# Two row-buffer slots of 16 batches in place of four of 8, in the plain gather passes of a graph network

## The chip, the cores and the metric

The program runs on one core of a Trainium2 chip. The metric is the device time of one execution in microseconds (us). The engines are called as in the profile: PE (TensorE, with PEld for its weight loads), DVE (VectorE), ACT (ScalarE), POOL (GpSimd) and SP (SyncE). PEq, POOLq and so on are the sequencers of these engines.

## What is computed

The reference runs four blocks on a graph of 12500 nodes and 200000 edges sorted by destination, with 128 features in fp32. Every block normalises its input, takes the positive part, and adds its result to `x`. What all of them share is a gather of source rows and a sum over destinations:

```python
def _L0_gnn_ref(x, edge_index, W0, b0, W1, b1, W2, b2):
    count = jax.ops.segment_sum(jnp.ones((src.shape[0],), dtype=x.dtype), dst, num_segments=n)
    inv = 1.0 / (count + 1.0)
    for W, b in ((W0, b0), (W1, b1), (W2, b2)):
        agg = jax.ops.segment_sum(x[src], dst, num_segments=n)
        neigh = agg * inv[:, None]
        x = jax.nn.relu(jnp.concatenate([x, neigh], axis=-1) @ W + b)
    return x
# L1: attention over the edges (softmax by destination), then a feed-forward block
# L2: segment_sum(relu(h[src] + edge_attr), dst), then two matmuls with batch norms
# L3: x + segment_sum(x[src] + edge_attr, dst)
```

## The kernel before

The sum over edges is the function `aggregate`, and the program calls it six times: `agg0`, `agg1` and `agg2` for the three layers of the first block, `agg3` for the attention, `agg4` for the third block (with edge attributes), and `agg5` for the last block. The calls `agg0`, `agg1`, `agg2` and `agg5` are the plain gather passes: rows are gathered from a table in HBM (`rows_a` or `rows_b`) and summed as they are. `agg3` reads rows that an earlier pass, `gat_gather`, has gathered on POOL and written to HBM; `agg4` gathers too, but adds edge attributes before the sum.

The 200000 edges are padded to 1568 batches of 128 edges. One batch is one indirect DMA, issued by POOL (line 680), that brings 128 rows of 128 numbers into `work`, one row per partition. Four batches form a group (`GT`). All edges of a group have destinations in one window of 64 nodes (`W`), so PE sums a group with four matmuls (line 751): the gathered rows are the weights, and a one-hot matrix of 128 edges by 64 nodes is the moving operand. DVE makes the one-hot matrices (`compare`, line 803) and adds each group's result from PSUM to `regionA` (`add`, line 846), at a column read from a table (line 837).

The loops run over 49 iterations (`NIT`) of 32 batches, which are eight groups. `work` holds the 32 batches of one iteration, and `S` says into how many slots it is divided; `ST` is the number of batches of a slot and `SG` that of its groups. The engines speak to each other per slot:

- POOL waits until PE has finished all `SG` groups of the slot in the iteration before (`summed[h]`, line 677), and then issues `ST` gathers. The wait and the increment of `moved` stand ahead of the slot's gathers in POOL's queue.
- PE waits for the one-hot matrices of the slot (line 741), for the landing of all its gathers (`gathered[h]`, line 743), and for each group for `added` (line 748): with `NB` banks of PSUM, a group can start when the group `NB` before it has been added. `NB` is 4 in the passes with a dense part (`agg0`, `agg1`, `agg2`, `agg5`) and 8 in `agg3` and `agg4`.
- DVE waits in `add` for each group's `summed[h]`, adds, and then makes the one-hot matrices of the same slot for the next iteration. In `agg0` it also sums the one-hot matrices (line 811) for the counts of edges.

`summed[h]` is incremented by PE once for each group, and both DVE and POOL wait for it. Semaphores carry the order across engines, and each engine runs its own list in order. When the sums of a chunk of 500 nodes are complete, `due_chunks` lets PE, DVE and ACT run the pass's dense part for this chunk (`Sage`, `Project` or `Finish`), between two iterations on PE, and on DVE between the last `add` and the last `compare` of an iteration. There are 25 chunks in a pass of 49 iterations.

Of the kernel before, what the change touches and what calls it, by code (L numbers as in the profile page):

```python
# [595 lines left out]
def aggregate(net, tag, table=None, extra=None, follow=None):  # L596
# [12 lines left out]
    attention, edges = extra == "attention", extra == "edges"  # L609
    width = XW if attention else D  # L610

    S = 2 if attention or edges else 4
    ST, SG = 2 * HALF // S, 2 * GPH // S
    rows = [net.work[:, h * ST * XW:h * ST * XW + ST * width] for h in range(S)]
    rows3 = [r.rearrange("p (t f) -> p t f", f=width) for r in rows]
    attr = [net.B[:, h * HALF * D:(h + 1) * HALF * D] for h in range(2)]

    piles = [net.C[:, REG + h * SG * W:REG + (h + 1) * SG * W] for h in range(S)]
    onehot = net.onehot[:, :, :, :].rearrange("p a t w -> p (a t) w")
# [12 lines left out]
    bank_of = lambda h, q, k: net.psum[0:high[k], (h * SG + q) % NB * 512 + k * W:(h * SG + q) % NB * 512 + (k + 1) * W]  # L632
    name = lambda k: [net.sem(f"{tag}_{k}{h}") for h in range(S)]
    index_ready = net.sem(f"{tag}_index")
    onehot_ready = name("onehot")
    gathered = name("gathered") if attention else [net.pool_sem() for _ in range(S)]
    summed = name("summed")
# [7 lines left out]
    with nc.Block() as block:  # L645
# [5 lines left out]
        if not attention:  # L651
# [12 lines left out]
            def _(pool):  # L664
# [3 lines left out]
                with pool.Fori(0, R) as r:  # L668
                    def gather(i, k):

                        n = pool.snap(r * NIT + i)
                        pool.wait_ge(index_ready, r * staged + i + 1)  # L672
                        for h in range(S):
                            if edges:
# [1210 lines left out]
def program(nc, dram, out):  # L1885
    with ExitStack() as ctx:
        net = Net(nc, ctx, dram)
        allocate(net)
        for step in (
                lambda: prepare(net),  # L1890

                lambda: normalise(net, "n0", first=True, table=net.TA),
                lambda: aggregate(net, "agg0", net.TA, "count",
                                  Sage(net, "sage0", "L0_gnn_W0", "L0_gnn_b0", net.TB, first=True)),
                lambda: aggregate(net, "agg1", net.TB, None,
                                  Sage(net, "sage1", "L0_gnn_W1", "L0_gnn_b1", net.TA)),
                lambda: aggregate(net, "agg2", net.TA, None, Project(net, "project")),

                lambda: gat_gather(net),
                lambda: gat_softmax(net),  # L1900
                lambda: gat_begin(net),
                lambda: aggregate(net, "agg3", extra="attention", follow=Shares(net, "shares")),
                lambda: gat_output(net),

                lambda: normalise(net, "n2", keep=True, table=net.TB),
                lambda: aggregate(net, "agg4", net.TB, "edges"),
                lambda: gin_output(net),

                lambda: normalise(net, "n3", table=net.TA),
                lambda: aggregate(net, "agg5", net.TA, None, Finish(net, "finish", out))):  # L1910
            with net.stage():
                step()
# [27 lines left out]
```

## Time and profile before

| | |
|---|---|
| time, median of 3 runs | 17063.85 us (16991.23 to 17120.43) |
| profiled execution | 16898.69 us, span of its instructions 16896.7 us |
| POOL busy | 9578.3 us (57%) |
| PE busy, PEld busy | 6796.4 us (40%), 5870.2 us (35%) |
| DVE busy, ACT busy | 3299.2 us (20%), 824.4 us (5%) |
| granted TensorE clock, mean | 0.529 of full speed |
| data moved | 1124.64 MB, mean 67 GB/s |

The stretches of the span, from the first gather of a pass to the start of what follows: `agg0` 296 to 2600 us, `agg1` 2600 to 4897, `agg2` 4897 to 7260, `gat_gather` 7299 to 9470, then the softmax, `agg3` from about 10235, the attention's output and a normalisation, `agg4` 11730 to 14260, and `agg5` 14618 to the end. The four plain passes are 9243 us of 16897. POOL is busy in each for about two thirds; the rest of its time is the gap between two gathers and the waits at the start of a slot. An average over the whole span hides this, since POOL does nothing in `agg3`.

### The profile page before, as it was taken

The page shows a single profiled execution, that of the slowest core. Times are in us where ns is not written, and L with a number is a line of the kernel's source. Part 1 is how long each engine was busy: PE and PEld are TensorE (multiplying, and loading weights), DVE is VectorE, ACT ScalarE, POOL GpSimd, SP SyncE. Part 2 cuts the span into 40 slices and gives each one's busy share as a digit, 9 for nine tenths or more (in the row PEclk, how much of TensorE's full clock was granted, in tenths as well). Part 3 has the DMA queues.
Part 4 walks back from the last instruction along what each step waited for, and adds up shares of the span by engine and source line. Part 5 has one row for each costly group of instructions (what it writes and reads, how often), then busy time and mean ns, then how long its engine had stood idle before and what let it go on. Part 6 is the DMA issues. An engine that isn't in the chain of part 4 may idle for free. (4 is left out here: it accounts for less than half of the span.)

```text
span 16896.7 us, 120575 instructions
## 1 busy us (share of the span) xinstructions
PE 6796.4 (40%) x30243; PEld 5870.2 (35%) x30244; DVE 3299.2 (20%) x6637; ACT 824.4 (5%) x1247; POOL 9578.3 (57%) x9860
## 2 busy tenths in 40 slices
PE   3444443333333444310000009996555555533333
PEld 2434333333333333200000008873555555333333
DVE  3222221111111222100000014444111112311111
ACT  1000000000000000000000000003000000200000
POOL 2666666666666666667777440001666664366666
PEclk8555555555555555555555555557555555655555
DMA  2111111111111222133333212222222222221212
GB/s 85 48 48 48 48 47 46 48 47 49 48 47 53 58 56 57 53 86 100 100 100 99 68 33 82 100 92 82 79 85 83 83 79 90 67 55 53 55 52 53
DMA packets 593156, 1124.64 MB, mean 67 GB/s; under 512 B 220826, under 2 KB 364385, under 8 KB 566579
## 3 DMA queue, kind: packets, MB, share of 16 engines
q0 software_dynamic: 307488, 624.42, 14.6%
q1 hardware_dynamic: 285622, 499.73, 8.8%
q8 instruction: 15, 0.25, 0.0%
q14 instruction: 31, 0.25, 0.0%
HBM read 904.32 MB, written 218.95 MB: 66 GB/s over the span
## 5 line engine op out<-in xcount | busy, mean ns | idle before, releaser
L680 POOL DMA_INDIRECT work<-rows_a,index x4704 | 4544.1, 966 | 2425.0 <-issue 1475.6
L751 PE MATMUL psum<-onehot,work 128*128 128x64 f32 x12544 | 2864.0, 416 | 3649.9 <-issue 1191.6
L680 POOL DMA_INDIRECT work<-rows_b,index x3136 | 3088.4, 985 | 1771.2 <-issue 1039.4
L751 PEld LDWEIGHTS psum<-onehot,work 128*128 128x128 f32 x12544 | 2721.0, 325 | 3797.5 <-issue 2795.1
L1191 POOL DMA_INDIRECT work<-attention_rows,index x1568 | 1608.7, 1026 | 610.6 <-issue 559.1
L751 PE MATMUL psum<-onehot,regionB 128*128 128x64 f32 x6272 | 1550.0, 417 | 720.8 <-issue 564.0
L751 PEld LDWEIGHTS psum<-onehot,regionB 128*128 128x128 f32 x6272 | 1438.7, 327 | 816.6 <-issue 789.8
L846 DVE TENSOR_TENSOR regionA<-regionA,psum 128x64 f32 x2352 | 508.7, 216 | 5116.3 <-remote 3598.3
L765 PE MATMUL psum<-onehot,regionB 128*4 128x64 f32 (+1 forms) x6272 | 1171.4, 358 | 467.2 <-issue 466.5
L765 PEld LDWEIGHTS psum<-onehot,regionB 128*4 128x4 f32 (+1 forms) x6272 | 1021.7, 224 | 516.9 <-issue 470.5
L182 POOL COPY work<-regionB 128x500 f32 (+1 forms) x75 | 45.3, 603 | 2030.6 <-DVE regionB L561 2030.6
L843 DVE TENSOR_TENSOR regionC<-regionC,psum 128x64 f32 (+1 forms) x1176 | 254.3, 216 | 3573.1 <-remote 2273.1
L1339 PE MATMUL psum<-ident,work 128*128 128x128 f32 x49 | 18.3, 452 | 2213.9 <-POOL work L1294 2213.7
L803 DVE TENSOR_TENSOR onehot<-rel_n,window 128x512 f32<-128x512 f32 (+1 forms) x980 | 779.4, 796 | 272.6 <-issue 263.3
L1339 PEld LDWEIGHTS psum<-ident,work 128*128 128x128 f32 x49 | 8.9, 182 | 2223.3 <-POOL work L1294 2220.9
L162 DVE CAST index<-src_n (+1 forms) x301 | 56.6, 189 | 2251.2 <-DMA work<-attention_rows,index 2073.2
L969 PE MATMUL psum<-regionB,weights 128*128 x100 | 101.5, 1118 | 790.1 <-DVE regionA L959 623.0
L831 DVE TENSOR_TENSOR regionB<-work,regionB 128x2048 f32<-128x2048 f32 x98 | 225.0, 2295 | 470.5 <-DMA regionB<-in_edge_attr 256.4
L661 ACT ACTIVATE regionB<-regionB 128x2048 f32<-128x2048 f32 x98 | 187.1, 1910 | 2383.8 <-DVE regionB L831 1808.8
L969 PEld LDWEIGHTS psum<-regionB,weights 128*128 128x128 f32 x100 | 25.1, 311 | 799.2 <-issue 799.2
L756 PE MATMUL psum<-regionC,ones 128*128 128x64 f32 x784 | 243.8, 404 | 135.6 <-issue 126.8
L1001 PE MATMUL psum<-ident,turn 128*125 128x128 f32 x300 | 77.7, 403 | 547.7 <-issue 306.5
(253 smaller groups left out, 4638.8 us busy)
## 6 DMA issues: line engine op xcount, KB each, us to landing
gathered_rows<-work SPq DMA_DIRECT2D x98, 1088.0 KB
work<-gathered_rows SPq DMA_DIRECT2D x98, 1088.0 KB, 4.9
regionB<-in_edge_attr SPq DMA_DIRECT2D x195, 512.0 KB
work<-rows_a,index POOLq DMA_INDIRECT x4704
work<-rows_b,index POOLq DMA_INDIRECT x3136
work<-attention_rows,index POOLq DMA_INDIRECT x1568
x_transposed<-regionA SPq DMA_DIRECT2D x75, 250.0 KB, 6.0
rows_a<-regionC SPq DMA_DIRECT2D x50, 250.0 KB
```

The costliest lines, as they stand in the source:

```text
L661: nc.scalar.activation(msgs[h], msgs[h], ACT.Relu).then_inc(relued[h], 1)
L680: pool.indirect_dma_start(rows3[h][:, t, :], None, table, bass.IndirectOffsetOnAxis(ap=net.index[:, k, h * ST + t:h * ST + t + 1], axis=0) ...
L751: last = nc.tensor.matmul(bank_of(h, q, 0), msgs3[h][:, t, 0:D], onehot[:, h * ST + t, :], start=(k == 0), stop=(k == GT - 1))
L756: last = nc.tensor.matmul(bank_of(h, q, 1), net.ones[:, :], piles[h][:, q * W:(q + 1) * W], start=True, stop=True)
L765: last = nc.tensor.matmul(bank_of(h, q, 1), lhs, onehot[:, h * ST + t, :], start=(k == 0), stop=(k == GT - 1))
L803: nc.vector.tensor_tensor(onehot[:, h * ST:(h + 1) * ST, :], net.rel_n[:, bass.ds(i * 2 * HALF + h * ST, ST)].unsqueeze(2) .broadcast_to([ ...
L831: nc.vector.tensor_tensor(msgs[h], rows[h], attr[h], ALU.add).then_inc(message[h], 1)
L843: nc.vector.tensor_tensor(Cc[0:high[1], bass.ds(at, W)], Cc[0:high[1], bass.ds(at, W)], bank_of(h, q, 1), ALU.add)
L846: nc.vector.tensor_tensor(A[:, bass.ds(at, W)], A[:, bass.ds(at, W)], bank_of(h, q, 0), ALU.add).then_inc(added, 1)
L969: net.nc.tensor.matmul(dense(net, 0), self.w[:, 0:D], net.col(net.B, c), start=True, stop=False)
L1001: t = net.nc.tensor.transpose(net.psum[0:SUB, (4 + k) * 512 + j * D:(4 + k) * 512 + (j + 1) * D], net.turn[:, j * SUB:(j + 1) * SUB], net. ...
L1191: pool.indirect_dma_start(rows3[h][:, t, :], None, net.XH, bass.IndirectOffsetOnAxis(ap=net.index[:, k, h * HALF + t:h * HALF + t + 1], ax ...
```

## The change

`S` is 2 in every call. It was 2 already in `agg3` and `agg4`, so the change is felt in the four plain passes alone:

```diff
@@ -609,7 +609,7 @@
     attention, edges = extra == "attention", extra == "edges"
     width = XW if attention else D
 
-    S = 2 if attention or edges else 4
+    S = 2
     ST, SG = 2 * HALF // S, 2 * GPH // S
     rows = [net.work[:, h * ST * XW:h * ST * XW + ST * width] for h in range(S)]
     rows3 = [r.rearrange("p (t f) -> p t f", f=width) for r in rows]
```

`ST` becomes 16 and `SG` 4. The batches, groups, matmuls, additions and PSUM banks stay. POOL's list in `agg1` (one iteration of the loop; the bracket names the semaphore that an instruction waits for) reads before:

```order
71 L677 ISA [waits agg1_index]
72 L680 DMA work<-rows_b,index 128x128 [waits agg1_summed0]
73 L680 DMA work<-rows_b,index 128x128 x7
74 L680 DMA work<-rows_b,index 128x128 [waits agg1_summed1]
75 L680 DMA work<-rows_b,index 128x128 x7
76 L680 DMA work<-rows_b,index 128x128 [waits agg1_summed2]
77 L680 DMA work<-rows_b,index 128x128 x7
78 L680 DMA work<-rows_b,index 128x128 [waits agg1_summed3]
79 L680 DMA work<-rows_b,index 128x128 x7
```

and in the changed kernel:

```order
59 L677 ISA [waits agg1_index]
60 L680 DMA work<-rows_b,index 128x128 [waits agg1_summed0]
61 L680 DMA work<-rows_b,index 128x128 x15
62 L680 DMA work<-rows_b,index 128x128 [waits agg1_summed1]
63 L680 DMA work<-rows_b,index 128x128 x15
```

Four waits for a slot of two groups have become two waits for a slot of four groups. The 32 gathers of an iteration stand in the same order.

On DVE, the one-hot matrices of a pass without counts, before the loop starts, as a difference:

```order
 L798 UNCONDITIONAL_BRANCH
 L798 ISA
-L803 TENSOR_TENSOR onehot<-rel_n,window 128x512 x4
+L803 TENSOR_TENSOR onehot<-rel_n,window 128x1024 x2
 L859 UNCONDITIONAL_BRANCH
 L859 ISA
```

Two comparisons of 1024 columns stand where four of 512 stood; in the loop each of them now follows four additions in place of two. In `agg0` the sum over the one-hot matrices (line 811) grows in the same way, from 128x128 results to 128x256. PE's list of instructions is the same; where PE waited for the gathers of 8 batches at every second group, it now waits for 16 at every fourth. SP clears fewer semaphores at the end of a pass (12 fewer after `agg0`).

## Rows read from the trace of the kernel before

**Rows 1.** Gathers (line 680) in agg0, agg1, agg2, agg4, agg5: the stretch, its length, POOL busy in them

```profile
296.00:2600.00 2304.00, 1537.37 (x1568) 0.51 0.18 47
2600.00:4897.00 2297.00, 1498.10 (x1568) 0.51 0.18 48
4897.00:7260.00 2363.00, 1503.35 (x1568) 0.52 0.20 54
...
11730.00:14260.00 2530.00, 1590.27 (x1568) 0.50 0.28 81
14618.00:16897.00 2279.00, 1503.38 (x1568) 0.50 0.20 54
```

**Rows 2.** Who waited for whom on POOL in agg0: us in total, times, longest

```profile
POOL work L680 <- remote: 269.6, 51, 6.9
```

**Rows 3.** The same for agg1

```profile
POOL work L680 <- remote: 277.0, 57, 7.5
POOL work L680 <- PE psum L751: 27.4, 9, 3.5
```

**Rows 4.** The same for agg2

```profile
POOL work L680 <- remote: 277.4, 47, 7.6
POOL work L680 <- PE psum L751: 107.8, 5, 26.5
```

**Rows 5.** The same for agg5

```profile
POOL work L680 <- remote: 235.6, 45, 7.6
POOL work L680 <- DMA regionC<-segment_ends: 49.4, 11, 7.5
```

**Rows 6.** Timeline of agg1: start, duration, engine, what, idle before

```profile
3051.29 0.94 POOL L680 DMA_INDIRECT work<-rows_b,index  x1 [0.30 <-issue]
3051.85 0.22 DVE L846 TENSOR_TENSOR regionA<-regionA,psum 128x64 f32 x1 [15.41 <-remote]
...
3056.82 0.22 DVE L846 TENSOR_TENSOR regionA<-regionA,psum 128x64 f32 x1 [4.75 <-remote]
3057.10 1.97 PE L751 MATMUL psum<-onehot,work 128*128 128x64 f32 x8 [3.00 <-DVE regionA L846]
...
3057.40 0.94 POOL L680 DMA_INDIRECT work<-rows_b,index  x1 [5.17 <-remote]
```

**Rows 7.** Timeline of agg3, where POOL issues nothing

```profile
10502.01 1.01 PE L765 MATMUL psum<-onehot,regionB 128*4 128x64 f32 x8
...
10503.24 0.21 DVE L843 TENSOR_TENSOR regionC<-regionC,psum 4x64 f32 x1 [2.50 <-PE psum L765]
```

**Rows 8.** Timeline of agg1 across two slot borders without a wait

```profile
3590.45 0.22 DVE L846 TENSOR_TENSOR regionA<-regionA,psum 128x64 f32 x1 [6.64 <-remote]
3590.59 0.69 DVE L803 TENSOR_TENSOR onehot<-rel_n,window 128x512 f32<-128x512 f32 x1
3590.76 1.34 POOL L680 DMA_INDIRECT work<-rows_b,index  x1 [0.30 <-issue]
...
3599.68 0.22 DVE L846 TENSOR_TENSOR regionA<-regionA,psum 128x64 f32 x1 [8.40 <-remote]
```

**Rows 9.** Timeline of agg2, after the dense part of a chunk

```profile
6083.24 4.55 PE L751 MATMUL psum<-onehot,work 128*128 128x64 f32 x32
...
6083.86 0.94 POOL L680 DMA_INDIRECT work<-rows_a,index  x1 [0.30 <-issue]
...
6090.37 0.22 DVE L846 TENSOR_TENSOR regionA<-regionA,psum 128x64 f32 x1 [10.04 <-remote]
...
6091.02 0.94 POOL L680 DMA_INDIRECT work<-rows_a,index  x1 [6.21 <-remote]
```

**Rows 10.** Groups by shape on DVE: the comparisons with 512 and with 1024 columns

```profile
L803 DVE TENSOR_TENSOR onehot<-rel_n,window 128x512 f32<-128x512 f32 x784 | 541.3, 691 | 212.8 <-issue 210.7 <-DVE base_now L792 1.0 <-DVE regionA L846 0.6
...
L803 DVE TENSOR_TENSOR onehot<-rel_n,window 128x1024 f32<-128x1024 f32 x196 | 238.1, 1215 | 59.8 <-issue 52.6 <-DVE base_now L792 2.0
```

**Rows 11.** Timeline at the end of agg5: the last gather and what follows

```profile
16873.17 0.94 POOL L680 DMA_INDIRECT work<-rows_a,index  x1 [0.30 <-issue]
16877.94 0.22 DVE L846 TENSOR_TENSOR regionA<-regionA,psum 128x64 f32 x1 [19.45 <-remote]
...
16878.22 3.67 PE L751 MATMUL psum<-onehot,work 128*128 128x64 f32 x16 [8.57 <-DMA work<-rows_a,index]
```

**Rows 12.** Passes with slots of 16: waits of POOL in agg4

```profile
POOL work L680 <- DVE regionB L831: 427.4, 31, 18.1
```

**Rows 13.** The same: gathers (line 1191) of gat_gather, stretch and busy

```profile
7299.00:9470.00 2171.00, 1608.74 (x1568) 0.50 0.35 100
```

## The prediction

> **What bounds the kernel now.** I read the page for the shares, then the busy time of POOL in stretches that I cut at the passes, then who waited for whom on POOL in each of these stretches, and last the timeline around some of the waits. The reader should see in the stretches [rows 1] that each plain pass takes 2279 to 2363 us, and that its 1568 gathers keep POOL busy for some 1500 us. One gather takes 0.94 us and the next starts 0.30 us after it [rows 6], so 1568 gathers one behind the other need 1568 x 1.245 = 1952 us. The clock that PE was granted is 0.50 to 0.52 of full speed in these stretches, its lower level of 1.2 GHz, and no engine but POOL is near full. POOL bounds the plain passes, and what stands above its 1952 us is mostly waiting at slot borders.
>
> The waits are 269.6 us in 51 waits in agg0 [rows 2], 277.0 + 27.4 = 304.4 us in 66 in agg1 [rows 3], 277.4 + 107.8 = 385.2 us in 52 in agg2 [rows 4], and 235.6 + 49.4 = 285.0 us in 56 in agg5 [rows 5]. That is 1244 us in 225 waits for 4 x 49 = 196 iterations: about one wait per iteration, though POOL has four borders in each.
>
> What they wait for is the odd part. PE needs only 1.97 us for a group (an fp32 matmul stands in the trace twice, so x8 is one group) [rows 6]. But the increment of `summed` arrives late. In agg3, where POOL is silent, DVE's addition starts 0.2 us after the matmuls of its group end [rows 7]. In agg1 DVE sat idle for 15.41 us and then 4.75 us before two additions, with PE doing nothing in between, and POOL sat idle for 5.17 us; the addition and POOL's next gather came within 0.6 us of each other [rows 6]. While POOL issues without a pause the increments come 6 to 15 us apart [rows 6, 8]; some 4.5 to 6 us after POOL has stopped they come together. In agg2 PE ran four groups from 6083.24 on, in 4.55 us; DVE's first addition of them is at 6090.37, after all four, and POOL restarts at 6091.02 after 6.21 us [rows 9]. So I read the plain passes as a cycle: POOL issues until it meets a border whose increments have not arrived, stands still for 5 to 6 us, everything outstanding is delivered, and it starts again. Why an increment is late while POOL issues, the trace doesn't show. I take it as a given.
>
> **The change part by part.** *The slack at a border.* Before, POOL asks at the border ahead of batch G for the group that was gathered 25 to 32 batches earlier; a slot of 8 leaves 24 gathers between the end of a slot and its reuse, 24 x 1.245 = 30 us. With slots of 16 it is 16 gathers, 20 us. At the first of the new borders POOL asks for groups 0 to 3 of the iteration, where it asked for 0 and 1; at the second for 4 to 7, where it asked for 4 and 5. The other two borders go, and with them a wait that was merged with an increment; across a border without a wait the gap was 0.30 us as everywhere [rows 8], so removing them gains nothing by itself.
>
> *The waits that result.* With 20 us of slack and 6 to 15 us between increments under a running POOL, four increments don't arrive in time, so every iteration has a wait. One is enough: it delivers all that is outstanding, and PE then works through the slot that has just landed while increments still come at once. I price this wait at 277.4 / 47 = 5.9 us, from agg2, where it already happens once an iteration at the same border [rows 4]. Its four groups there were delivered together [rows 9], so asking for four and not two costs nothing more. 48 x 5.9 = 283 us per pass. Against the present waits: agg0 +14, agg1 -21, agg5 -2. In agg2 the long dense part (`Project`, after about every second iteration) sets when PE can turn to the slots, so I leave its 385.2 us as it is. Sum -9 us.
>
> *Waits at the second border.* Where groups 6 and 7 come too late after a restart, POOL waits again. My estimate for agg1 and agg5 is three borders in ten: the first increments after a restart come at once, and each of the rest 6.6 to 8.4 us apart [rows 8], so that two late ones still fit into 20 us and three don't. In agg0 and agg2 the dense part is longer and covers it. 2 passes x 48 x 0.3 x 5.9 = 170 us. A wait at the second border makes the next one at the first border unlikely, since everything has just been delivered, so I take half, +85 us. The bounds are 0 and one wait at every border in all four passes, 4 x 48 x 5.9 = +1133 us.
>
> *Longer comparisons on DVE.* A gather that starts while DVE compares takes 1.34 us and not 0.94 [rows 8]. In all, busy time exceeds 1568 x 0.944 = 1480 us by 57 in agg0, 18 in agg1, 23 in agg2 and 23 in agg5 [rows 1]. A comparison of 1024 columns takes 1.215 us, one of 512 takes 0.691 [rows 10]. Both the chance to meet a gather and the time lost grow with the length, so half as many comparisons cost (1.215 / 0.691)^2 / 2 = 1.55 times as much: +31, +10, +13 in agg0, agg1, agg5, and nothing in agg2, where POOL waits anyway. Sum +54 us. If the loss grew in proportion to the length, it would be 0.88 of today's, -12 us. The Trainium skill has a rule for this (SBUF — State Buffer, the part on the shared port pair): a VectorE operation with two SBUF inputs and a GpSimd operation that reads SBUF exclude each other, and whoever comes second waits for the whole of the other. The trace agrees in kind, 0.40 us lost beside a comparison of 0.69. If every comparison held a gather for its full length, the total would be 98 x 1.215 = 119 us per pass against 196 x 0.691 = 135, and the change would save 64 us in the four passes. This estimate by the page stands outside my sum.
>
> *The end of a pass.* The last slot's groups follow the last landing: 16 matmuls in 3.67 us for two groups [rows 11]; now four groups, +3.7 us, four times, +15 us. PE's first group of a pass starts 10 us later, which nothing waits for. Fewer semaphores to clear: under 1 us each pass, taken at nothing.
>
> Sum: -9 + 85 + 54 + 15 = +145 us. On the profiled execution, 16898.7 us, that gives 17044. The median of the runs is 165 us above the profiled execution; I carry the difference over to it: 17064 + 145 = 17209, given as **17200 us**, 0.8% slower.
>
> **The rivals.** *A wait at every border.* If increments of groups 4 to 7 are late after a restart as well, POOL stands still twice per iteration. For it: the 6.64 and 8.40 us between increments only 10 to 20 us after a restart [rows 8]. Against it: agg0 and agg2 wait once per iteration now and pass three borders freely. Price: half to all of +1133 us in place of the 85, so 17064 - 9 + 567 to 1133 + 54 + 15, which is 17690 to 18260 us. It decides as soon as the last four groups take over 20 us from the restart. The edge pass has slots of 16 and takes 2530 us [rows 1], with 427.4 us in 31 waits of up to 18.1 us [rows 12]; but its slots are freed by DVE behind eight more additions. Plain passes of its stretch would give 4 x 2530 in place of 9243 us [rows 1], +877, which is 17941.
>
> *Fewer or shorter waits: faster.* gat_gather also has slots of 16, and its stretch is 2171 us, with gathers that are no shorter (1608.7 us busy) [rows 13], since what frees its slots is no increment by PE. If long runs without a border disturbed PE's increments less, the plain passes could fall toward that. All the way it is 4 x 2171 against 9243 us [rows 1], -559 us, 16505 us. Halfway, or with waits as short as 4.5 us (48 x 1.4 x 3 passes = 200 us less), it is 16830 to 17000 us. Against it: the slack is smaller at every second border and nowhere larger.
>
> *No effect.* The cycle sets its own length: agg1 with 66 waits, agg5 with 56 and agg0 with 51 take 2297, 2279 and 2304 us [rows 1], so the number of borders may not matter. The lateness might also belong to the profiling, and then the timed runs wouldn't have it. Against that: the profiled execution is not slower than the timed ones. Time: 17064 plus 0 to 60, up to 17120 us.
>
> **How the numbers follow.** A measurement of this kernel tells about 1% from no change; 1% is 16893 and 17235 us. Chances: the forecast, one wait per iteration with some second ones (17080 to 17330), 0.45; no effect 0.25; more second waits without reaching every iteration (17330 to 17690) 0.12; a wait at every border 0.06; fewer or shorter waits 0.12, of which 0.08 below 16893. Slower by over 1%: 0.12 + 0.06 + nearly half of the forecast's case, 0.20, makes 0.38. Faster by over 1%: 0.08. Within: 0.54. The range from 16960 to 17600 leaves out a good half of the faster case, the waits at every border and the worst of the case before it, and takes in the runs' own spread of about 0.4% either way.
>
> **What would show it.** Right: in agg1 and agg5 48 to 65 waits of POOL, of 5 to 6 us, at the first border of the iterations; POOL's busy time in a plain pass up by about 10 us (30 in agg0); agg2 unchanged within 20 us; DVE's additions in bursts of four or more after each wait. Wrong: about 96 waits a pass, or waits over 10 us because PE hasn't run the groups when POOL stops (additions that PSUM's four banks wait for); or under 40 waits. If the passes are equal in the profile but the times differ, the lateness is the profile's own.

## The result

The changed kernel takes 16946.9 us (median of 20 runs, 16901.6 to 16979.6), the kernel before 17111.1 us (20 runs, 16904.3 to 17367.7). The ratio is 0.9947, with a 95% interval of 0.9924 to 0.997: half a per cent faster, where 0.8% slower was forecast. The ratios here and below compare only runs within 1.5% of the fastest of their kernel, which leaves out eight of the 20 runs of the kernel before; the ratio of the two medians over all runs is 0.9904. The medians hide the more telling difference. The runs of the kernel before lie over a range of 463 us, those of the changed kernel over 78 us; and the execution whose trace stands ahead of the prediction, 16898.7 us, was faster than any of the 20.

So the two profiled executions stand the other way round: the changed kernel's took 16957.4 us, 59 more. Of its trace, the gathers in agg0, agg1, agg2 and agg5 (stretch, length, POOL busy; they answer to [rows 1]):

```profile
292.00:2617.00 2325.00, 1529.26 (x1568) 0.51 0.18 47
2617.00:4920.00 2303.00, 1524.51 (x1568) 0.51 0.18 48
4920.00:7286.00 2366.00, 1529.51 (x1568) 0.52 0.20 54
14655.00:16955.00 2300.00, 1528.70 (x1568) 0.50 0.20 53
```

Who waited on POOL in agg1 (answers to [rows 3]; `remote` means that an increment ended the wait, but that no instruction of this core ended shortly before it; `issue` means that the view knows of nothing that was waited for):

```profile
POOL work L680 <- issue: 524.8, 1520, 37.4
POOL work L680 <- remote: 262.3, 48, 6.4
```

and in agg2 (answers to [rows 4]):

```profile
POOL work L680 <- issue: 518.8, 1519, 29.8
POOL work L680 <- remote: 239.2, 43, 6.7
POOL work L680 <- PE psum L751: 83.5, 6, 24.6
```

The reader sees the cycle of the prediction: 48 waits in agg1, once an iteration, 262.3 / 48 = 5.5 us each, where there were 66. Agg2 has 322.7 us of waits in place of 385.2. The timeline of agg2 shows how it goes (it answers to [rows 9]):

```profile
6363.44 0.22 DVE L846 TENSOR_TENSOR regionA<-regionA,psum 128x64 f32 x1 [6.14 <-remote]
6364.13 0.95 POOL L680 DMA_INDIRECT work<-rows_a,index  x1 [5.88 <-remote]
...
6364.68 1.23 DVE L803 TENSOR_TENSOR onehot<-rel_n,window 128x1024 f32<-128x1024 f32 x1
6365.38 1.35 POOL L680 DMA_INDIRECT work<-rows_a,index  x1 [0.30 <-issue]
...
6368.43 0.22 DVE L846 TENSOR_TENSOR regionA<-regionA,psum 128x64 f32 x1 [0.71 <-DVE regionA L846]
...
6370.34 0.68 DVE L1093 TENSOR_TENSOR regionA<-regionA,regionC  x1 [1.69 <-issue]
```

POOL's wait ahead of batch 0 ends at 6364.13, the additions of the whole iteration are done 5 us later, and at 6370.34 the dense part begins. POOL has issued only 5 of the 32 gathers (40 us) that stand between its restart and its next question at this border. A gather beside the comparison takes 1.35 us.

The trace holds one more thing, which no term of the prediction has. Once in 112 gathers POOL stands still for about 2 us between two gathers of 0.94 us, and the view names nothing that it waited for. In agg1, where no comparison ran at the time:

```profile
2780.83 0.94 POOL L680 DMA_INDIRECT work<-rows_b,index  x1 [0.30 <-issue]
2782.27 3.03 PE L751 MATMUL psum<-onehot,work 128*128 128x64 f32 x13 [19.42 <-DMA work<-rows_b,index]
2783.94 0.94 POOL L680 DMA_INDIRECT work<-rows_b,index  x1 [2.16 <-issue]
2784.50 0.22 DVE L846 TENSOR_TENSOR regionA<-regionA,psum 128x64 f32 x1 [17.20 <-PE psum L751]
```

Counted from 0, the gathers 113, 225, 337 and so on of every plain pass have such a gap ahead of them: 13 in a pass, 24 us together. Every traced plain pass with two slots has all 13, on every chip; with four slots at most two of these places have a gap over 1 us, and in `odd` below none has. The trace of the kernel before already had them in `gat_gather`, which has slots of 16, at the same places:

```profile
7438.87 0.94 POOL L1191 DMA_INDIRECT work<-attention_rows,index  x1 [0.31 <-issue]
7441.94 0.94 POOL L1191 DMA_INDIRECT work<-attention_rows,index  x1 [2.13 <-issue]
```

What POOL does in them, no view shows.

### The profile page after: what moved, and what is told of

Same layout as the page of the kernel before. It is cut to its first block and busy times, and to the rows that moved or that the text cites. A ratio compares the mean times of both kernels' runs of the same rounds, so it can differ in the third digit from the quotient of the medians.

```text
span 16955.6 us, 119259 instructions
## 1 busy us (share of the span) xinstructions
PE 6756.4 (40%) x30243; PEld 5863.6 (35%) x30244; DVE 3233.9 (19%) x6147; ACT 824.7 (5%) x1247; POOL 9653.8 (57%) x9860
## 5 line engine op out<-in xcount | busy, mean ns | idle before, releaser
L751 PE MATMUL psum<-onehot,work 128*128 128x64 f32 x12544 | 2822.4, 419 | 4459.8 <-DMA work<-rows_a,index 2818.1
L803 DVE TENSOR_TENSOR onehot<-rel_n,window 128x1024 f32<-128x1024 f32 x588 | 717.9, 1221 | 244.7 <-issue 225.0
L756 PEld LDWEIGHTS psum<-regionC,ones 128*128 128x128 f32 x784 | 214.2, 328 | 77.7 <-issue 77.7
```

Source lines behind the costliest of these rows:

```text
L751: last = nc.tensor.matmul(bank_of(h, q, 0), msgs3[h][:, t, 0:D], onehot[:, h * ST + t, :], start=(k == 0), stop=(k == GT - 1))
L756: last = nc.tensor.matmul(bank_of(h, q, 1), net.ones[:, :], piles[h][:, q * W:(q + 1) * W], start=True, stop=True)
L803: nc.vector.tensor_tensor(onehot[:, h * ST:(h + 1) * ST, :], net.rel_n[:, bass.ds(i * 2 * HALF + h * ST, ST)].unsqueeze(2) .broadcast_to([ ...
```

## The experiments

A step is the time from the start of one gather to the start of the next; without a wait it is 1.249 us. The tables of this section give, for a pass, the time from its first to its last gather in the trace, then the waits as count/sum (the steps over 3.5 us, less 1.249 us each), and as "long" the steps over 9 us. The kernels ran on five chips. A kernel is compared with runs of the kernel before on the same chip, taken between its own. Three of the chips (5, 13 and 7) are "late": there PE's increments reach DVE and POOL late while POOL issues, as in the trace ahead of the prediction. Two (2 and 0) are "prompt": the increments come at once.

**Three executions of one kernel.** Two further traces of the kernel before, unchanged, on chip 5.

> The kernel before, unchanged: one more execution with a trace, because the first one (16898.7 us) is faster than 19 of 20 timed executions (16904 to 17368 us, median 17111). Theory A (irregular cycle): with four slots the waits at the borders fall differently from execution to execution, and a slower execution has more or longer waits of POOL in agg0, agg1, agg2 and agg5; the waits of the four passes, 1244 us in the first trace, grow by as much as the time does, and agg4 and the gather pass of the attention stay within 20 us. Theory B (from outside): the spread comes from somewhere else, for instance slower gathers or transfers; then the 0.944 us of a gather, or agg4 and the attention's pass, change as well.

> The kernel before, unchanged, a third trace. As for the second: by theory A whatever it is slower than 16899 us lies in POOL's waits in the four plain passes; by theory B it is spread over all passes. If all three traces agree within 30 us in every pass, neither is supported.

They took 16914.9 and 17095.3 us.

```
          total     agg0        agg1        agg2                agg4        agg5
first     16898.7   2277 49/262 2260 60/277 2349 51/370 5 long  2511 32/421 2254 50/261
four_a    16914.9   2273 50/257 2261 56/275 2359 51/378 5 long  2523 34/433 2256 50/264
four_b    17095.3   2289 50/275 2257 53/271 2493 58/517 11 long 2544 34/456 2257 52/263
```

Of the 180 us between the last two, 134 lie in agg2, 16 in agg0, 21 in agg4 and 27 between agg4 and agg5 (some stretches are shorter); a gather alone stays at 0.94 us. Theory A holds, but for agg2 alone, and not for the whole of the difference. The waits in agg2 of four_b, from its trace:

```profile
POOL work L680 <- issue: 486.1, 1508, 26.8
POOL work L680 <- PE psum L751: 274.1, 11, 27.1
POOL work L680 <- remote: 261.5, 49, 7.0
```

There are eleven waits that end with a matmul, 25 us each, where [rows 4] has five. A timeline around one of them shows where it comes from:

```profile
5217.93 0.22 DVE L846 TENSOR_TENSOR regionA<-regionA,psum 128x64 f32 x1 [1.37 <-PE psum L751]
5219.49 0.22 DVE L846 TENSOR_TENSOR regionA<-regionA,psum 128x64 f32 x1 [1.34 <-issue]
...
5253.30 0.22 DVE L846 TENSOR_TENSOR regionA<-regionA,psum 128x64 f32 x1 [20.78 <-remote]
5255.22 0.68 DVE L1093 TENSOR_TENSOR regionA<-regionA,regionC  x1 [1.70 <-issue]
...
5278.67 3.28 DVE L1109 RECIPROCAL regionA<-regionA  x1 [3.77 <-ACT regionA L1159]
...
5284.35 2.18 PE L1139 MATMUL psum<-weights,turn 128*125 128x136 f32 x8 [6.63 <-ACT regionA L1164]
5286.33 6.92 PE L751 MATMUL psum<-onehot,work 128*128 128x64 f32 x32
...
5290.65 0.94 POOL L680 DMA_INDIRECT work<-rows_a,index  x1 [27.08 <-PE psum L751]
```

The additions of the iteration's groups 4 and 5 are at 5217.93 and 5219.49, as POOL starts the next iteration (5219.4). The last one, of group 7, comes at 5253.30, with a wait of POOL ahead of batch 24. Only then can the dense part begin (5255.22); PE is back at the groups at 5286.33, and POOL, long through its slots, has stood still for 27 us. The dense part takes 31 us here. In the changed kernel's timeline above it begins 6 us after POOL's restart and lies under the gathers.

The other dense parts of agg2 say the same. In each of the three traces 24 of them are followed by a question of POOL ahead of batch 0. Of these 72, 51 begin when POOL has started batch 5 of an iteration, and the wait that follows is 5.3 to 6.2 us. The other 21 begin at batch 13 to 25, and the wait that follows is 17.8 to 27.0 us. In the changed kernel's trace 21 begin at batch 3 to 6 (waits of 4.0 to 6.5 us) and three at batch 16 to 18 (20.6 to 24.2 us).

**The same slack in two phases.** What the change does to POOL's questions alone can be had with four slots for PE and DVE, if POOL asks for two slots at once: ahead of batches 0 and 16 (`pairs`), or ahead of 8 and 24 (`odd`). The edits against the kernel before:

```diff
# pairs:
-                                pool.wait_ge(summed[h], n * SG + SG)
+                                if h % 2 == 0:
+                                    pool.wait_ge(summed[h + 1], n * SG + SG)
+                                    pool.wait_ge(summed[h], n * SG + SG)
# odd:
-                                pool.wait_ge(summed[h], n * SG + SG)
+                                if h % 2 == 1:
+                                    pool.wait_ge(summed[h], n * SG + SG)
+                                    pool.wait_ge(summed[(h + 1) % S], (n + (h + 1) // S) * SG + SG)
```

> Four slots of 8 for PE and DVE, but POOL asks for two slots at once at every second border (the slack of slots of 16, with the comparisons and additions of slots of 8). Theory A: the order that POOL waits in makes the change: the time is that of the changed kernel, 16950 us within 30, with a spread under 100 us, about 48 waits a pass at the first border. Rival (the longer but fewer operations of DVE, or PE's wait for 16 batches, make the change): it stays like the kernel before, about 17100 us, spread over 300 us.

On chip 5: 16836.4 us (4 runs, 16825.8 to 16855.8), the kernel before 17307.5 (16956.4 to 17393.7), ratio 0.9893 (0.979 to 0.9997). The range is 30 us and each plain pass has 48 waits ahead of batch 0, as theory A has it, but the time is 114 us under the 16950 that it gave: the changed kernel has costs that pairs has not, as chip 13 shows below.

> Four slots of 8, POOL asks for two slots at once as in pool_asks_pairs, but at the two other borders (ahead of batches 8 and 24 of an iteration, not 0 and 16): the same slack and the same number of questions, half a slot pair out of phase. Phase theory (what counts is whether POOL's wait comes at the end of an iteration, so that group 7 is added and the dense part of a chunk can begin at once): the waits fall at batches 8 and 24, group 7 comes late in every iteration with a chunk, agg2 has 20 or more waits of over 20 us, and the kernel takes 17250 to 17500 us, with a small spread. Slack theory (only the number of gathers between question and landing counts): the time is that of pool_asks_pairs, 16836 us within 40.

That run met chip 2, a prompt one; it follows below. Again, side by side on chip 13:

> pool_asks_odd once more. On a prompt chip 15399 us within 20 again. On a late chip it decides between phase and slack: phase theory, agg2 with 20 or more waits of over 20 us and 17250 to 17500 us; slack theory, 16836 us within 40.

> pool_asks_pairs once more. On a late chip 16836 us within 40 again. On a prompt chip: only POOL's question differs from the kernel before, so agg0, agg1 and agg5 are as before (1975 to 1980 us between first and last gather) and agg2 has about 24 waits of 8 us: 15154 + 200 = 15350 us within 40. If the comparisons of 1024 columns and not the question made agg2 long, it stays at 15154.

> The changed kernel, unchanged, to see it beside the kernel before on whatever chip this is. On a chip where PE's increments come late while POOL issues (chip 5 so far): 16947 us within 40, the kernel before at 17000 to 17400 and spread. On a chip where they come at once (chip 2, where the kernel before took 15154 us): no waits in agg0, agg1 and agg5, gathers beside comparisons stretched (+53, +45 and +27 us, as the traces of four_agg2_only and four_but_agg2 showed against each other), and in agg2 some 24 waits of 8 us behind the dense part (+215 us): 15490 us within 40, 2.2% slower than before.

```
chip 13             median    range               ratio (interval)          agg2
kernel before       16959.0   16792.5 to 17143.0
odd                 17140.4   17131.6 to 17164.2  1.0114 (1.0024 to 1.0203) 2627 49/642 24 long
changed kernel      16832.9   16810.6 to 16853.7  0.9935 (0.9896 to 0.9974) 2320 48/287  3 long
pairs               16723.8   16709.7 to 16746.8  0.9870 (0.9782 to 0.9957) 2253 48/273  0 long
```

Waits on POOL in agg2, of odd and then of pairs:

```profile
POOL work L682 <- PE psum L753: 513.3, 24, 35.1
POOL work L682 <- issue: 488.8, 1516, 26.9
POOL work L682 <- remote: 144.1, 28, 6.3
```

```profile
POOL work L682 <- issue: 490.8, 1519, 28.2
POOL work L682 <- remote: 244.5, 41, 6.3
POOL work L682 <- PE psum L753: 43.5, 7, 6.9
```

Slack and number of questions are equal, and the two differ by 417 us, 374 of them in agg2. The phase theory's main sign is there, 24 long waits, one for each dense part but the last; its sizes were too large, since 14 of the 24 are of 13 to 19 us, where over 20 was expected, and the time of 17140 is below 17250. The slack theory had the two kernels equal and falls. The other three passes of odd (2277, 2243, 2245) are within 20 us of those of pairs (2258, 2243, 2243).

Two things lie in these 374 us. In odd the dense part begins 20 to 27 us after POOL's restart (37 in one case), in pairs 5 to 6 us after it (9 in one case): that is the late group 7 of the phase theory. But odd also asks at batch 24 for the groups that PE does right behind the dense part, 10 us sooner than pairs asks for them. On the prompt chips, where the dense part begins at batch 5 in both, odd's agg2 takes 2251 us with 24 waits of 11 us, and agg2 with POOL asking in pairs 2089 and 2090 us (table below). So about 160 of the 374 us need no late increment, and some 210 go with the lateness.

Beside each other on chip 13, pairs and the changed kernel also show what two slots cost PE and DVE with POOL's questions the same: 109 us. In the changed kernel the waits of the four plain passes are 73 us shorter, but their gathers take 77 us more, and the gaps between gathers, which are nearly all those once in 112, 99 us more.

Chips of the late kind differ as well: pairs is 113 us faster on chip 13 than on chip 5, and the changed kernel 114 us faster than in the first measurement. The forecasts that carried a time over (16836 and 16947 within 40) missed by that much; only kernels on one chip are compared here.

**One part alone.** `S = 4` in all plain passes but agg2, or in agg2 alone, as edits of the changed kernel:

```diff
-    S = 2
+    S = 2 if attention or edges or tag == "agg2" else 4   # four_but_agg2
+    S = 4 if tag == "agg2" else 2                         # four_agg2_only
```

> Four slots in agg0, agg1 and agg5, two in agg2, once more. On a prompt chip 15366 us within 20. On a late chip: if agg2 holds the spread, all runs are within 100 us and the median is 16900 us within 30; if agg0's dense part can fall into long waits too, single runs lie 50 us or more above.

> Four slots in agg2 alone, once more. On a late chip, if agg2 holds the spread of the kernel before: range over 150 us, single runs over 17000 us, and in its trace the agg2 pass holds the waits over 9 us; if not, range under 60 us. On a prompt chip 15298 us within 20.

Two slots in agg2 and four elsewhere (chip 13): 16789.2 us, range 35, ratio 0.9933 (0.990 to 0.9965); 44 us under the changed kernel; 16900 within 30 was expected. Four in agg2 alone (chip 7): 16956.8 us, range 137, ratio 1.0004 (0.9972 to 1.0036), agg2 2399 us with 11 waits over 9 us (a range over 150 us was expected); the changed kernel beside it:

> The changed kernel beside the kernel before. On a late chip 16830 to 16950 us, within 50 of each other, the kernel before spread over 250 us or more. On a prompt chip 15490 us within 40, 2.2% slower than the kernel before: the three passes with a light dense part +125 us together by stretched gathers, agg2 +215 us by about 24 waits of 8 us.

16832.3 us, range 59, ratio 0.9934 (0.9902 to 0.9966), agg2 2323. The kernel before has a range of 266 us beside these two, over more runs. With two slots in agg2 the spread is gone (35 us), with four in agg2 alone half of it is there (137 us). The gain is agg2's alone.

**Fewer increments.** The changed kernel with two increments per iteration in place of eight. The main edit (the waits of POOL and DVE count slots accordingly, which is left out here):

```diff
-                            last.then_inc(summed[h], 1)
+                            if SI == SG or q == SG - 1:
+                                last.then_inc(summed[h], 1)
```

> The changed kernel, with `summed` incremented once for each slot of four groups in the plain passes, not once for each group: 2 increments of PE per iteration in place of 8. If each increment costs its own 6 to 15 us while POOL issues (a queue of increments), two fit into the 20 us of slack, the waits go from about 48 a pass to under 10, and the time falls by up to 4 x 250 = 1000 us, to about 16000. If the increments are held back as long as POOL issues whatever their number, the waits stay at 48 a pass, DVE's additions come later, and the time is 16950 to 17100 us.

17546.6 us on chip 5, ratio 1.0308 (1.0198 to 1.0418), outside both forecasts. Agg1 has 48 waits of 264 us in all, where the changed kernel's trace has 48 of 248 us, so the lateness is no matter of the number of increments. But additions can now start only when a whole slot is signalled, and the dense part is late in nearly every iteration with a chunk (in agg2 21 of 24 begin at batch 18 to 26), though POOL waits ahead of batch 0: agg2 2712 us with 23 long waits, agg0 2508 us with 15.

**Less data.**

> quarter_rows on another chip (a quarter of each row gathered in the plain passes, POOL asking in pairs). On a prompt chip as there, 15320 us. On a late chip it tells what PE's increments are late for: if for the data moved, the waits of agg1 and agg5 vanish and these passes take under 2000 us; if for the issuing by POOL or the number of descriptors, 47 to 49 waits of 5 to 7 us stay.

Chip 7, 16831.9 us (one execution). The kernel leaves out three quarters of each row, so it doesn't compute the same result. It moves 816 MB in place of 1125, and agg1 takes 2246 us with 48 waits of 259 us, as with whole rows (pairs on chip 13: 2243, 48 of 276). Its waits:

```profile
POOL work L684 <- issue: 516.1, 1520, 51.6
POOL work L684 <- remote: 273.9, 48, 7.5
```

The lateness doesn't go with the bytes. Whether it goes with POOL's issuing, the descriptors or the DMA increments stays open.

**Chips without late increments.** Four kernels met chip 2, where the kernel before takes 15154.5 us (15142.7 to 15164.9), and two met chip 0, where it takes 15165.4 (15144.8 to 15175.2).

> Four slots in agg2 alone, two in the other plain passes. If the spread of the kernel before (16904 to 17394 us) is the number of long waits in agg2, about 20 us each, this kernel keeps the spread, with single runs over 17100 us and a range of more than 200 us, and its trace has between 5 and 25 waits over 9 us in agg2. If the spread comes from the other passes, it is within 100 us.

> Four slots in agg0, agg1 and agg5, two in agg2. If agg2 holds the spread: all runs within 100 us of each other, and since the three passes were 13 to 17 us shorter each with four slots in the traces, the median is 16900 us within 30, under the 16947 of the changed kernel. If agg0's dense part can fall into long waits too, single runs lie 50 us or more above.

> pool_asks_pairs, but in the plain passes each gather brings 32 of the 128 columns of a row (128 bytes, not 512; the other columns are zero, and the gathers of a pass start after this is written, up to 30 us later): a quarter of the data with the same number of gathers, rows and increments. If PE's increments are late because of the data that the DMA engines move, the waits of POOL shrink below 3 us or vanish, and a plain pass goes toward 1568 x 1.249 = 1958 us plus 20. If they are late because POOL issues (or makes the descriptors), the waits stay at 47 to 49 a pass of 5 to 7 us.

> The changed kernel beside the kernel before, a third time, for a chip without late increments: there 15490 us within 40, 2.2% slower than the kernel before. On a late chip 16830 to 16950 us, 0.5 to 0.7% faster.

> Four slots everywhere, POOL asking in pairs in agg2 alone. If agg2's phase is all that there is to gain, this has the time of pool_asks_pairs: on a late chip 110 us under the changed kernel within 30, with a range under 60 us. If POOL's question in pairs also helps agg0, agg1 and agg5, it is slower than that by 30 us or more. On a prompt chip 15350 us, the wait behind the dense part.

```
                 chip  median   ratio (interval)          agg0  agg1  agg2                agg5
odd              2     15398.9  1.0164 (1.0147 to 1.0181) 1977  1976  2251 24 waits/270   1977
four_agg2_only   2     15298.2  1.0099 (1.0082 to 1.0116) 2028  2023  2011  5 waits/17    2006
four_but_agg2    2     15365.8  1.0140 (1.0123 to 1.0157) 1975  1978  2226 24 waits/198   1979
quarter_rows     2     15320.2                            1971  1971  2090 22 waits/118   1972
changed kernel   0     15500.4  1.0224 (1.0207 to 1.0241) 2030  2026  2200 24 waits/189   2008
pairs_agg2_only  0     15235.7  1.0044 (1.0028 to 1.0061) 1977  1980  2089 21 waits/106   1982
```

There the change costs 2.2%. Increments come at once: in the changed kernel's trace on chip 0 the additions follow the matmuls at their pace,

```profile
3010.52 0.22 DVE L846 TENSOR_TENSOR regionA<-regionA,psum 128x64 f32 x1 [12.14 <-PE psum L751]
3012.19 0.22 DVE L846 TENSOR_TENSOR regionA<-regionA,psum 128x64 f32 x1 [1.45 <-PE psum L751]
3013.90 0.22 DVE L846 TENSOR_TENSOR regionA<-regionA,psum 128x64 f32 x1 [1.48 <-PE psum L751]
```

With four slots agg0, agg1 and agg5 take 1975 to 1982 us, near the 1958 us that 1568 steps of 1.249 us make. With two slots (four_agg2_only against four_but_agg2) they take 53, 45 and 27 us more, 125 together. Gathers held up by comparisons are 48 us of this, and the gaps once in 112 gathers are 77. In four_but_agg2's agg2, which has two slots:

```profile
5001.41 1.23 DVE L803 TENSOR_TENSOR onehot<-rel_n,window 128x1024 f32<-128x1024 f32 x1 [1.72 <-issue]
5001.47 1.99 POOL L680 DMA_INDIRECT work<-rows_a,index  x1 [0.30 <-issue]
```

a gather beside a comparison takes 1.99 us, 1.05 more than alone. The other part is agg2. In the changed kernel's trace on chip 0 PE is back from the dense part some 42 us after POOL has started batch 0 of the iteration, POOL asks for groups 0 to 3 after 40 us, and waits 189 / 24 = 8 us each time (17 us in all with four slots, where it asks for 0 and 1). The forecast for this chip's kind, 15490 us, written before the run, met 15500. Asking in pairs in agg2 alone gave 78 us of agg2's 189 us (2089 and 2200 against 2011), so the kernel took 15236 us where I had expected 15350. The other 111 us (2200 against 2089) come with the slots of 16 on PE and DVE, and the two traces divide them: 83 us are longer waits, 14 us longer gathers, 14 us more gaps between gathers. The waits are longer because the dense part begins at batch 8 and not 5, 3.5 us later: PE starts the last four groups of an iteration only when all 16 of their batches have landed.

## Why the prediction was wrong

*What held.* The cycle itself, on the chips with late increments: 48 waits a pass, about one per iteration, of 5.5 us (5.9 forecast), 45 of the 48 in agg1 at the first border. Agg1 went from 66 waits to 48. The first term, -9 us, measured between the two traces by the steps over 3.5 us, is -2 in agg0, -29 in agg1 and -21 in agg5. The end of a pass (last gather to the next first gather, or to the end) is 2 to 4 us longer, 11 us in the four passes, where 15 was forecast.

*Waits at the second border* (+85 us forecast) came to half of it: 17 us in agg1 and 26 in agg5. After a restart PE had signalled all four groups of the slot within 20 us nearly always.

*Longer comparisons* (+54 us). The busy time of the gathers changed by -8, +26, +26 and +25 us in agg0, agg1, agg2 and agg5, together +70, where +31, +10, 0 and +13 stood. The sum came near by luck: agg0 lost nothing, and agg2, costed at nothing "where POOL waits anyway", lost as much as the others. Why agg0 lost nothing stays open. The prediction took 0.40 us as the loss beside a comparison, which is what a gather beside one of 512 columns shows [rows 8]; the gather of 1.99 us beside one of 1024 lost 1.05. The Trainium skill's rule (SBUF — State Buffer, on the shared port pair: a VectorE operation with two SBUF inputs and a GpSimd operation that reads SBUF can't run together, and the later of the two is held until the other has finished) fits both gathers, while the prediction's side estimate, a full comparison lost each time, does not: the comparison had 0.52 us left to run when the first gather began and 1.17 us when the second did, and each gather lost 0.12 us less than that.

*A term that was missing.* The gaps once in 112 gathers, 24 us a pass, cost 79 us net in the four passes, since agg1 and agg5 of the kernel before had some 20 us of other gaps. The prediction had no term for them, though `gat_gather`, its example of a pass with slots of 16 [rows 13], shows them. Steps under 3.5 us grew by 15, 42, 53 and 38 us, +148 with the longer gathers, where +54 was forecast.

*The step that failed* is the sentence "I leave its 385.2 us as it is", with the one that carried the 165 us between the trace and the median over unchanged. They are one error: both take the time of agg2 for a constant. Agg2's waits measured 308 us in place of 370 between the traces (steps over 3.5 us), -62 where 0 stood, and they differ from run to run. With four slots POOL's wait can settle ahead of batch 24, or ahead of batch 0. In the first phase group 7 is late, the dense part starts late, and POOL pays 12 to 21 us more per dense part; in the second it is hidden. The trace had 5 long waits in agg2 ([rows 4], the line with 107.8 us in 5), four_b 11; the median of the 20 runs is 212 us above the trace, which at 20 to 24 us each (four_b has six more than four_a, and its agg2 takes 134 us more) would be about ten more. This last number is an estimate, since no trace was taken of such a run. Two slots put POOL's wait ahead of batch 0 in nearly all iterations; three long waits are left. The change loses some 60 us against a lucky execution of the kernel before (its profiled one) and wins 160 against its median.

In numbers: the forecast was +145 us on the profiled execution and as much on the median. Between the profiled executions it is +59: the waits of the plain passes -114 (forecast -9 + 85), the shorter steps +148 (forecast +54), the ends of the passes +11 (forecast 15), 14 us elsewhere. Between the medians it is -164. The difference of 223 us is the carry-over: the median lies 212 us above the profiled execution in the kernel before (165 was carried for both kernels) and 10 us below it in the changed kernel. The sign that agg2 would be unchanged within 20 us came true, 2366 us after 2363, but by luck: 62 us less of waits against 53 us more of longer steps. One slip in the rivals' sums changes nothing else: halfway between 17064 and 16505 is 16784 us, not 16830.

The rivals all asked how many waits there would be and how long. None asked at which place of the iteration they stood with respect to the dense part, though [rows 9] showed a good phase and the line with 26.5 us in [rows 4] a bad one. The spread of the three runs, 129 us, was taken for noise; by the runs with two slots in agg2, whose range is 35 us, it is the mechanism.

On the prompt chips the forecast has the right sign by luck, and is too small (2.2% slower). No wait per iteration comes there; 189 us are agg2's, where the dense part meets the shorter slack, a price that no row of the trace before could show, and some 125 us are longer gathers and gaps in the other three passes.

A version that beats both kernels on the chips with late increments is pairs: 1.3% under the kernel before and 109 us under the changed kernel on chip 13. On the prompt chips the kernel before is the fastest that ran.

## What to carry to other kernels

Before a cost is read from one trace, the spread of the timed runs deserves a question of its own: where a kernel's runs differ by 1% and more while those of another version agree within 0.5%, look for a wait that can settle in two places, and take a second and third trace of the same kernel. The size of a buffer slot sets the slack, but also where in the loop the one inevitable wait falls; place it right ahead of the work that must start early. If the trace has a part that already runs in the changed form, as `gat_gather` did here, its gaps deserve a look too, and not only its total. And a change that is worth 1% should be seen on more than one chip.

## What was not expected of the hardware

The kernel before takes 15.15 to 15.17 ms on two of the chips (2 and 0) and 16.96 to 17.31 ms on three others (5, 13, 7; medians). The granted clock is nearly the same, 0.532 to 0.538 of full speed on the former and 0.525 to 0.529 on the latter. By the traces some 1200 us of the difference lie in the plain passes with four slots (7.9 ms for the four on a prompt chip, put together from four_but_agg2 and four_agg2_only, and 9.1 ms in the trace of the kernel before). On the late chips PE's increments, seen by DVE and POOL, come late while POOL issues indirect DMAs, and 4 to 6 us after it stops. In agg1, agg2 and agg5 DVE's additions start up to 33 us after the last matmul of their group in the trace of the kernel before, and at most 2.4 us after it in that of the changed kernel on chip 0. The lateness depends neither on the number of increments (once_per_slot) nor on the bytes (quarter_rows_again). It is not the whole of the difference: `gat_gather`, which doesn't use PE, takes 2165 to 2169 us against 1979 to 1984, with POOL busy for 1609 us in the trace of the kernel before and 1479 us in that of the changed kernel on chip 0, and agg4 takes 2458 to 2544 us against 2173 to 2192. What makes these chips late was not found; whether the profiler's recording has a part in it was not tried.

POOL's gap of about 2 us once in 112 gathers, in all passes whose slots have 16 batches and not in those with slots of 8, was not expected either. What makes it was not found.
